# Layer 1's projection in three 16-bit products, whole chunks in the feed-forward, and layer 1's weights loaded in pieces

## The reference

```python
xn = _layernorm(x, axis=-1)                       # of layer 0's output
Xn = (X - mu) * jax.lax.rsqrt(var + LN_EPS) * ln_w + ln_b
qkv = jnp.einsum('bsd,df->bsf', Xn, W_in)         # 256 -> 768, three of 256
gate, up = silu(W_gate x), W_up x                 # 256 -> 704 each
return _qlinear(gate * up, wq_down, s_down)       # 704 -> 256
```

## Time and profile before

| | us |
|---|---|
| median of 3 runs | 1011.3 |
| the profiled execution | 1011.56 |
| its span, first to last instruction | 1009.8 |
| PE busy | 921.3 |
| DVE busy | 806.2 |
| ACT busy | 674.1 |
| POOL busy | 710.9 |
| layer 1's first instruction, from the span's start | 653.80 |

### The profile page before, as it was taken

The page is one execution under the profiler, slowest core; times in us unless marked ns, Lnnn a source line. Parts: engine busy times, 40 slices in busy tenths (PEclk is TensorE's granted clock), DMA queues, the critical chain, the costliest instruction groups (busy, mean ns, idle before and its releaser), DMA issues. The chain is left out here.

```text
span 1009.8 us, 26174 instructions
## 1 busy us (share of the span) xinstructions
PE 921.3 (91%) x8671; PEld 502.9 (50%) x8671; DVE 806.2 (80%) x1632; ACT 674.1 (67%) x1747; POOL 710.9 (70%) x1019
## 2 busy tenths in 40 slices
PE   5677998998998998999998998599999999999998
PEld 2455665666665766766766765342222222222223
DVE  6797878688787788787787776578999999999971
ACT  3555656556656656666566565217999999898995
POOL 4678889799899799799899877522866766544231
PEclk8798999999999999999999999779999999999999
DMA  7555645444445454445444445252221212323101
GB/s 241 107 107 125 114 96 87 95 100 90 98 96 86 92 99 87 99 100 90 96 95 93 80 93 98 59 143 66 53 43 25 37 38 46 53 49 53 33 6 43
DMA packets 253114, 83.61 MB, mean 83 GB/s; under 512 B 227316, under 2 KB 251572, under 8 KB 252724
## 3 DMA queue, kind: packets, MB, share of 16 engines
q1 hardware_dynamic: 249284, 76.43, 38.5%
q10 hardware_dynamic: 3696, 5.51, 2.0%
HBM read 18.49 MB, written 4.19 MB: 22 GB/s over the span
## 5 line engine op out<-in xcount | busy, mean ns | idle before, releaser
L1347 DVE TENSOR_REDUCE l_mxv<-l_mx 128x1 f32<-128x1024 f32 x256 | 295.0, 1215 | 20.5 <-PE l_mx L1567 20.1
L1267 ACT ACTIVATE l_prob<-l_sc 128x512 f32<-128x512 f32 x512 | 278.4, 598 | 18.5 <-PE l_sc L1575 15.5
L420 ACT ACTIVATE an<-an 128x256 f16<-128x256 f32 x128 | 53.3, 417 | 177.6 <-DVE an L613 177.0
L760 POOL TENSOR_TENSOR tt<-tt 128x320 f32<-128x320 f32 x128 | 115.0, 898 | 76.9 <-DVE tt L678 76.8
L1521 PE MATMUL l_acc<-l_prob,qkv_all 128*17 128x256 f32 x2048 | 161.0, 387 | 3.0 <-DVE l_acc L1330 0.5
L1567 PE MATMUL l_mx<-early 48*128 48x512 f16 x512 | 156.4, 387 | 4.1 <-DVE l_mxv L1347 2.2
L1575 PE MATMUL l_sc<-early 50*128 50x512 f16 x512 | 154.8, 383 | 0.1
L751 POOL TENSOR_TENSOR rm<-ss,half_neg 128x5 f32<-128x5 f32 x128 | 154.6, 1207 | 0.0
L889 PE MATMUL qk<-early,xh 128*128 128x384 f16 x512 | 129.8, 336 | 3.4 <-issue 3.1
L678 DVE TENSOR_TENSOR tt<-qk,tcw 128x640 f32<-128x640 f32 x128 | 105.0, 820 | 18.4 <-POOL nat L770 9.3
L420 ACT ACTIVATE nat<-tt 128x128 f16<-128x128 f32 (+1 forms) x256 | 78.3, 355 | 50.0 <-POOL tt L780 49.8
(11 more groups left out here) (184 smaller groups left out, 1961.7 us busy)
## 6 DMA issues: line engine op xcount, KB each, us to landing
qkv_all<-w_qkv SPq DMA_DIRECT2D x3, 768.0 KB, 9.0
v<-v SPq DMA_DIRECT2D x64, 32.5 KB, 1.9
xn_all<-xs SPq DMA_DIRECT2D x16, 128.5 KB, 2.1
xa<-x SPq DMA_DIRECT2D x16, 128.0 KB, 2.3
tk<-nat SPq DMA_TRANSPOSE x128, 2.8
qkv_all<-w_o ACTq DMA_DIRECT2D x8, 256.0 KB, 3.1
ats<-an SPq DMA_TRANSPOSE x128, 2.4
xc<-x SPq DMA_DIRECT2D x16, 128.0 KB, 2.2
```

Of the source, the lines that this page charges most:

```text
L420: return act.activation(dst, src, ACT.Copy, scale=scale)
L760: pool.tensor_tensor(t1[:, b, :, :].rearrange("p h (a d) -> p h a d", a=2), t1[:, b, :, :].rearrange("p h (a d) -> p h a d", a=2), tt[:, b ...
L1267: act.activation(prob[:, (y * NI + u) % NPR, h * 512:(h + 1) * 512], sc[:, k % NSC, :], ACT.Exp, scale=D1 ** -0.5).then_inc(s_["act_sc"], 1)
L1347: dve.tensor_reduce(mxv[:, x % 2, u:u + 1], mx[:, MX[k] % 2, :], AX.X, ALU.max).then_inc(s_["dve_mx"], 1)
```

## The change

`win` becomes `wi_hi` and `wi_lo`, two 16-bit parts (times 64) that ACT and DVE make in slots 19 to 24 (`WI_AT`) from `wi_f`, which now lies in the staging space. `xt1` becomes `xt1h`, which ACT writes, and `xt1l`, which DVE writes; ACT's copy moves from the end of its slot to a place ahead of the exponential. Each 32-bit product of the projection becomes three 16-bit products, and ACT's copies of the results scale by 1/64. The feed-forward's weights and `ht` are padded with zeros to 768, and PE uses whole chunks. The three broadcast rows are loaded in slots 13, 14 and 15, the two halves of the weight in slots 16 and 17. The fill of ones moves to slot 26. GpSimd still makes the queries' low part. The semaphores of the output weights' split are shared with the new one.

```diff
+WI_AT = 2 * G + 3
-        gu_hi = sb("gu_hi", [P, 2, KC, HID], F16)
+        gu_hi = sb("gu_hi", [P, 2, KC, NF * P], F16)
-        win = sb("win", [P, KC, 3 * D])
+        wi_hi = sb("wi_hi", [P, KC, 3, D], F16)
+        wi_lo = sb("wi_lo", [P, KC, 3, D], F16)
-        xt1 = sb("xt1", [P, KC, P])
+        xt1h = sb("xt1h", [P, KC, P], F16)
+        xt1l = sb("xt1l", [P, KC, P], F16)
...
@@ sync @@
-                if s == 2 * G:
-                    sp.dma_start(win[:, :, :], w_in).then_inc(l1w_ld, 16)
-                    sp.dma_start(lnw[:, :], ln_w.broadcast_to([P, D])).then_inc(l1w_ld, 16)
-                    sp.dma_start(lnb[:, :], ln_b.broadcast_to([P, D])).then_inc(l1w_ld, 16)
-                    sp.dma_start(wr[:, :], w_r.broadcast_to([P, D])).then_inc(l1w_ld, 16)
+                for at_slot, dst, src in ((2 * G - 3, lnw, ln_w), (2 * G - 2, lnb, ln_b), (2 * G - 1, wr, w_r)):
+                    if s == at_slot:
+                        sp.dma_start(dst[:, :], src.broadcast_to([P, D])).then_inc(l1w_ld, 16)
+                for c in range(KC):
+                    if s == 2 * G + c:
+                        sp.dma_start(wi_f[:, c, :], w_in[:, c, :]).then_inc(l1w_ld, 16)
@@ scalar, behind the copy to xh and ahead of the exponential @@
+                n = on_way(s, 1)
+                if n is not None:
+                    act.wait_ge(s_["pe_xat"], n + 1)
+                    ev(xt1h[:, :, :], extra[:, 0:D].rearrange("p (k t) -> p k t", k=KC)).then_inc(s_["act_xat"], 1)
@@ scalar, behind the output weights' split @@
+                j = s - WI_AT
+                if 0 <= j < 3 * KC:
+                    act.wait_ge(l1w_ld, 16 * (3 + KC))
+                    ev(wi_hi[:, j // 3, j % 3, :], wi_f[:, j // 3, j % 3 * D:(j % 3 + 1) * D], WS).then_inc(s_["act_wo_win"], 1)
-                n = on_way(s, 1)
-                if n is not None:
-                    act.wait_ge(s_["pe_xat"], n + 1)
-                    ev(xt1[:, :, :], extra[:, 0:D].rearrange("p (k t) -> p k t", k=KC)).then_inc(s_["act_xat"], 1)
...
-                    ev(qk1_all[:, n % B, n // B, :], extra[:, :]).then_inc(s_["act_l1"], 1)
+                    ev(qk1_all[:, n % B, n // B, :], extra[:, :], 1 / WS).then_inc(s_["act_l1"], 1)
@@ vector @@
+            for w in (gu_hi, gu_lo):
+                dve.memset(w[:, :, :, HID:], 0.0)
+            dve.memset(ht[HID - NF * P:, NF - 1, :, :], 0.0)
...
+                j = s - WI_AT
+                if 0 <= j < 3 * KC:
+                    dve.wait_ge(s_["act_wo_win"], G + j + 1)
+                    dve.scalar_tensor_tensor(wi_lo[:, j // 3, j % 3, :], wi_f[:, j // 3, j % 3 * D:(j % 3 + 1) * D], WS,
+                                             wi_hi[:, j // 3, j % 3, :], ALU.mult, ALU.subtract).then_inc(s_["dve_wo_win"], 1)
@@ vector, behind ss and xl @@
+                n = on_way(s, 1)
+                if n is not None:
+                    dve.wait_ge(s_["act_xat"], n + 1)
+                    dve.tensor_tensor(xt1l[:, :, :], extra[:, 0:D].rearrange("p (k t) -> p k t", k=KC), xt1h[:, :, :],
+                                      ALU.subtract).then_inc(s_["dve_xt1"], 1)
@@ gpsimd @@
-                if s == LAG_W + NF:
+                if s == WI_AT + 3 * KC + 1:
...
@@ tensor @@
+            def layer1_product(dst, parts):
+                for c in range(KC):
+                    for j, (a, w) in enumerate(((xt1h, wi_hi), (xt1h, wi_lo), (xt1l, wi_hi))):
+                        ins = pe.matmul(dst, a[:, c, :], w[:, c, parts, :],
+                                        start=(c == 0 and j == 0), stop=(c == KC - 1 and j == 2))
+                ins.then_inc(s_["pe_l1"], 1)
...
-                    cols, m = chunk(f)
+                    cols = slice(f * P, (f + 1) * P)
-                                ins = pe.matmul(ff[0:m, u, :, :], w[:, u, c, cols], a[:, i % 2, c, :, :],
+                                ins = pe.matmul(ff[:, u, :, :], w[:, u, c, cols], a[:, i % 2, c, :, :],
-                        ins = pe.matmul(ob[:, 0:D], ht[0:rows, f, n % B, :], wd[0:rows, f, :], start=False, stop=(k == G - 1))
+                        ins = pe.matmul(ob[:, 0:D], ht[:, f, n % B, :], wd[:, f, :], start=False, stop=(k == G - 1))
...
-                    pe.wait_ge(s_["act_xat"], n + 1)
+                    pe.wait_ge(s_["dve_xt1"], n + 1)
                     if n == 0:
-                        pe.wait_ge(l1w_ld, 16 * 4)
-                    for c in range(KC):
-                        ins = pe.matmul(extra[:, :], xt1[:, c, :], win[:, c, 0:2 * D], start=(c == 0), stop=(c == KC - 1))
-                    ins.then_inc(s_["pe_l1"], 1)
+                        pe.wait_ge(s_["dve_wo_win"], G + 3 * KC)
+                    layer1_product(extra[:, :], slice(0, 2))
```

More of the change, by code:

```diff
@@ L302, in layer0 @@
         sd_b = stage[:, o2 + NF * D:o2 + NF * D + D]
+        o3 = o2 + NF * D + D
+        wi_f = stage[:, o3:o3 + KC * 3 * D].rearrange("p (k c) -> p k c", k=KC)
         def landed(eng, m):
@@ L519, in _ @@
                     ev(vv1_all[:, n % B, n // B, :, 0:D1],
-                       (qk[:, 0, 0:D] if n >= NT - 2 else extra[:, 0:D]).rearrange("p (h e) -> p h e", h=H1)).then_inc(s_["act_l1"], 1)
+                       (qk[:, 0, 0:D] if n >= NT - 2 else extra[:, 0:D]).rearrange("p (h e) -> p h e", h=H1), 1 / WS
+                       ).then_inc(s_["act_l1"], 1)
                 n, k, ok = at(s, LAG_T)
@@ L803, in _ @@
                     ins.then_inc(s_["pool_tcw"], 1)
-                if s == LAG_W + NF:
+                if s == WI_AT + 3 * KC + 1:
+                    pool.wait_ge(s_["dve_gu"], NF)
                     pool.wait_ge(s_["dve_wd"], NF)
-                    pool.memset(vv1_all[:, :, :, :, D1:VW].rearrange("p b i h e -> p (b i h) e"), 1.0
-                                ).then_inc(s_["pool_ones"], 1)
+                    pool.wait_ge(s_["dve_wo_win"], G + 3 * KC)
+                    pool.memset(vv1_all[:, :, :, :, D1:VW].rearrange("p b i h e -> p (b i h) e"), 1.0)
                 n = s // G - 2
@@ L813, in _ @@
                     if n == 0:
-                        pool.wait_ge(l1w_ld, 16 * 4)
+                        pool.wait_ge(l1w_ld, 16 * (3 + KC))
                     pool.wait_ge(s_["dve_xa"], n + 1)
@@ L922, in _ @@
                     n = NT - 2
-                    pe.wait_ge(s_["act_xat"], n + 1)
-                    for c in range(KC):
-                        ins = pe.matmul(extra[:, :], xt1[:, c, :], win[:, c, 0:2 * D], start=(c == 0), stop=(c == KC - 1))
-                    ins.then_inc(s_["pe_l1"], 1)
+                    pe.wait_ge(s_["dve_xt1"], n + 1)
+                    layer1_product(extra[:, :], slice(0, 2))
                     pe.wait_ge(s_["act_A"], NT * G)
                     pe.wait_ge(s_["dve_A"], NT * G)
-                    for c in range(KC):
-                        ins = pe.matmul(qk[:, 0, 0:D], xt1[:, c, :], win[:, c, 2 * D:3 * D], start=(c == 0), stop=(c == KC - 1))
-                    ins.then_inc(s_["pe_l1"], 1)
+                    layer1_product(qk[:, 0, 0:D], slice(2, 3))
                 n, k, ok = at(s, LAG_W)
@@ L938, in _ @@
                     if n == 0:
-                        pe.wait_ge(s_["dve_wo"], k + 1)
+                        pe.wait_ge(s_["dve_wo_win"], k + 1)
                     for j in range(2):
@@ L945, in _ @@
                     if 0 <= f < NF:
-                        rows = chunk(f)[1]
                         pe.wait_ge(s_["dve_h"], n // B * NF + f + 1)
@@ L983, in _ @@
                         pe.wait_ge(s_["act_l1"], n * 2 + 1)
-                    for c in range(KC):
-                        ins = pe.matmul(qk[:, 0, 0:D] if last else extra[:, 0:D], xt1[:, c, :], win[:, c, 2 * D:3 * D],
-                                        start=(c == 0), stop=(c == KC - 1))
-                    ins.then_inc(s_["pe_l1"], 1)
+                    layer1_product(qk[:, 0, 0:D] if last else extra[:, 0:D], slice(2, 3))
         return wq_ld, [*gu_ld, wd_ld]
```

16 lines of the change are left out of this document (8 added, 8 removed).

## The result

The changed kernel takes 999.22 us on the median of 20 runs (995.51 to 1014.09), the kernel before 1010.5 beside it (20 runs): a ratio of 0.9883, interval 0.9860 to 0.9905. In a second series beside the kernel before the ratio was 0.9902 (0.9873 to 0.9931). The profiled execution took 997.62 us, 13.9 us less than that of before, with a span of 995.8. Seven of the changed kernel's 20 runs and two of the 20 before took 10 to 15 us longer than the others, which the ratio mostly leaves out; over all runs the means differ by 8.2 us.

The account below looks back on a forecast made before the run. TensorE and GpSimd were taken to bound the kernel in turns, with TensorE leading at the projections. 6.4 + 1.6 + 3 - 1 + 0.3 = 10.3 us off 1011.56 gave 1001.3 us, range 994 to 1008.

Parts of the forecast that it names:

- Projection: Slots 5, 6, 13 and 14: three 16-bit products save 0.70 us a tile over tiles 0 to 13, 9.8 us.
- Wait for the low part: Slots 5 and 13: PE's projection waits for DVE's new subtraction, losing 3.4 us over tiles 0 to 13.
- Chunk of the first products: Slot 14: a padded sixth feed-forward chunk saves 0.23 us, seven times beside the first, 1.6 us.
- Down product: Slots 0 and 8: padding 64 rows gains nothing under POOL's cover; without that cover some 3 us.
- Pieces: Slots 13 to 17: spreading the load burst wins back 3 us, bounds 5.6 gained to 2 lost.
- Splits: Slots 19 to 24: six ACT copies and six DVE subtractions for the weight cost 1 us, bounds 0 and 4.
- Tail: Tiles 14 and 15, the last of a layer: projection savings less the later start, 0.3 us gained.
- POOL did not become the bound: Rival that POOL takes over, making projection and chunk worth nothing: 1009.3 us; chance 0.16 together with an ineffective change.
- rival 2: Slots 5 and 13: projection caught behind DVE's product, which waits for POOL's low part; slower, 1019.9 us, chance 0.05.
- rival 3: Slot 3: PE's stall lengthens and brings half clock in seven rounds, costing 8.5 us; 1009.8 us, chance 0.05.
- Rival 4: Better: low-part waits of 3.4 us vanish in later slack and the burst's 5.6 us return; 995.3 us, chance 0.09.

Follow-up runs that it names:

- e1: The kernel before with whole, zero-padded chunks in both feed-forward loops and nothing else; ratio 0.9957 (0.9905 to 1.0008).
- e5: The kernel before with only the down product always taking 128 rows; its one execution took 1021.94 us.
- e6: The changed kernel with layer 1's weight and the three rows loaded in one burst at slot 16; lead over the kernel before 1.3 us at slot 20.
- e3: The changed kernel with chunks of 64 and one load burst at slot 16, so the three-product projection alone; ratio 0.9910 (0.9869 to 0.9951).
- e9: The changed kernel plus matmuls that feed no result, keeping TensorE at work between the layers; 998.30 us, ratio 0.9874.
- e4: The changed kernel with the activations' high and low parts made earlier in their slot, on ACT and DVE; ratio 0.9892 (0.9831 to 0.9952).
- after_again: The changed kernel run once more, unaltered, beside two variants on one chip; 1000.01 us, ratio 0.9902.
- e10: e4 plus matmuls that feed no result, keeping TensorE at work between the layers; 989.72 us, ratio 0.9807 against the kernel before.

## Why the prediction was right, and where its terms were off

The forecast was 1001.3 us. The mechanism held: both projections lie where PE leads, and what PE saves there moves what follows. The profiled executions differ by 13.9 us against 10.3 forecast, the medians by 11.3. That the sum came so close is in part luck: three of its terms were off, in both directions, and the one for the pieces depends on a clock that falls in some executions only. Term by term:

- **Projection, 9.8.** Right: 0.52 and 0.21 us a tile at the forecast spacing, 10.1 in all.
- **Wait for the low part, -3.4.** Mis-sized a little, 4.6 (10.7 now, 6.1 for ACT before). In six of thirteen tiles it is 0.59 us, the 0.46 that was there plus the 0.13 forecast. The longest are tiles 2 and 10 with 1.69 and 1.53. In tile 2 DVE comes without a pause from the slot before, and in both the two-input subtraction of `an` takes 0.81 us (its median is 0.43). The rows are tile 2's:

```profile
212.52 0.81 DVE L683 TENSOR_TENSOR an<-an 128x256 f16<-128x256 f32 x1
213.26 0.81 DVE L697 TENSOR_TENSOR tt<-qk,tcw 128x640 f32<-128x640 f32 x1
213.99 0.47 DVE L703 TENSOR_REDUCE ss<-sq 128x5 f32<-128x325 f32 x1
214.39 0.41 DVE L717 TENSOR_TENSOR xt1l<-extra,xt1h 128x256 f16<-128x256 f32 x1
```

- **Chunk of the first products, 1.6.** Right: 0.23 us a round in e1.
- **Down product, 0.** This is the step that failed: "where POOL goes without a pause: I cost it at nothing". Slots 0 and 8 got shorter by 0.35 and 0.19 us in every round of e5, which kept 2.4 to 2.6 us of it, near the 3 that the prediction gave without that cover; e1's execution kept less, so the size is open. POOL's lack of pauses in a slot didn't mean that PE waits for it there; the waits of PE for keys, most of them at slots 3 and 4, were the view to ask, and in e5 they grew by 0.8 us only (22.9 us from 100 to 600 us, 22.1 before). In slot 8 the narrow product starts 0.20 us behind the one ahead of it and the pv 0.63 behind it, in e5 0.11 and 0.53, so the loss lies on both sides of it. The Trainium skill's TensorEngine Tiling (Array Packing) page (Key Properties) says that changing the tiling mode drains TensorE, without a price; the later starts fit that, but no run here shows the drain itself.
- **Pieces, 3.** Some 1.7 by e6 and by all traces at slot 20; 2.5 at layer 1's start is within the scatter. Half of what the trace showed at that place was a half clock that e1 and e3 didn't have with the same burst.
- **Splits, -1.** Mis-sized: 2.1 at slot 32, since the price of an instruction was too low; at layer 1's start 0.4, which the scatter there hides.
- **Tail, 0.3.** 0.9 from slot 128 to layer 1 (12.1 to 13.0).

With these, 10.1 - 4.6 + 1.6 + 2.4 + 2.5 - 0.4 + 0.9 = 12.5 of the 13.0 us at layer 1's start. That they meet so well shows little, as the same kernel again had 14.8. What whole chunks add to three products is less than the 1.6 and 2.4 us of this sum: from slot 20 to layer 1 e3 gains 8.4 us, and the four executions that have whole chunks too (the changed kernel twice, e9 and e6) 9.2 to 12.1; their waits for the low part are larger, 9.7 to 11.0 us against 8.8. Layer 1 itself, the same code, was 1.0 us shorter (354.7 against 355.6) with less half clock.

The rivals: POOL did not become the bound (its waits are still 24.4 us). DVE's wait for POOL's low part, on which rival 2 rests, came five times, at slots 2 and 3 and never at a projection; the waits over 1.3 us in tiles 2 and 10 have another source, the long `an`. The stall of rival 3 came, 3.00 us until 459.76 with 0.73 of full clock in the four us from 459, but in no more rounds than before. Rival 4's time, 995.3, is nearer to the profiled execution than the forecast is, for another reason: its waits did not vanish.

## What to carry to other kernels

An operand's new low part should be made as early as its input allows, not where its neighbour in the code stands: the same instruction ahead of five others, with ACT's copy moved up too, was worth some 9 us, against 11 for the whole change. A partly filled tile took longer here than a padded one (0.19 to 0.35 us a product), and whether TensorE leads in a slot is read from TensorE's waits, not from how busy another engine is there. A price halved from the mean of a larger instruction can miss: the eight behind the mean of the earlier trace rows take from 0.68 to 1.21 us, the four longest ending 0.55 us behind the end of a GpSimd operation, and such a wait doesn't halve with the columns. And one trace of a kernel is not enough to price a term of 1 or 2 us where the same kernel again differs by as much.

## What the runs showed of the hardware that was not expected

A down product of 64 rows takes longer than one of 128: 0.19 us in slot 8 and 0.35 in slot 0, the same in every round (e5). TensorE can be at 0.50 of its clock for 24 us in which it is busy 24.00 (e4), so steady work did not raise it there, while in other executions of the same instructions it rose; and a stall of some 3 us was followed by the lower level in one execution (3.17 us in e6) and not in the next (3.39 in e1), as was one of some 2 us (2.08 in after_again, but not 2.46 in e10).
